# Token gathers of three graph layers in quarters of TensorE's array, two tiles at a time

## The reference, cut to what matters

```python
# layer 0: attention, 8 heads of 64
dots = where(m2, q @ k.T / 8, -big)
attn = 0.33 * softmax(dots) + 0.33 * adj + 0.33 * exp(-dist)     # masked; adj serves as dist too
x = LN(x + (attn @ v) @ W_out + b_out)
# layer 1: mean over neighbours
x = LN(x + relu(concat[x, (adj @ x) / deg] @ W.T))
# layer 2: two hypergraph convolutions, G = Dn * H @ (Be * H.T), H = (adj != 0)
h = LN(relu(G @ (x @ W1.T) + b1)) * gamma + beta
x = LN(x + (G @ (h @ W2.T) + b2 + x))
# layer 3: gated attention
xg = x * sigmoid(deg * Wd + bd)
s = (QK @ QK.T / 16) * adj,  QK = sigmoid(xg @ Wqk.T + bqk)
x = LN(x + relu((s / (sum(s) + 1e-6)) @ xg @ Wl.T + bl + xg @ Wr.T))
```

## Time and profile before

| | value |
|---|---|
| median of 3 runs | 1185.15 us |
| profiled execution, its own time | 1184.85 us |
| span of its instructions | 1182.8 us |
| TensorE (PE) busy | 1127.0 us, 95% |
| DVE busy | 919.8 us, 78% |
| ACT busy | 595.7 us, 50% |
| POOL busy | 572.5 us, 48% |

### The profile page before, as it was taken

The page is one execution under the profiler, slowest core; times in us unless marked ns, Lnnn a source line. Parts: engine busy times, 40 slices in busy tenths (PEclk is TensorE's granted clock), DMA queues, the critical chain, the costliest instruction groups (busy, mean ns, idle before and its releaser), DMA issues.

```text
span 1182.8 us, 29171 instructions
## 1 busy us (share of the span) xinstructions
PE 1127.0 (95%) x10416; PEld 951.4 (80%) x10416; DVE 919.8 (78%) x2223; ACT 595.7 (50%) x1266; POOL 572.5 (48%) x731
## 2 busy tenths in 40 slices
PE   5889999999999999999999999999999999999875
PEld 4768888888888888888888888888888888888763
DVE  6675887878788887878877788788778878777865
ACT  2536465454646445474544647454464645546331
POOL 2426356382644628264472735537273553826341
PEclk9899999999999999999999999999999999999897
DMA  7010102010010201001020100102001010100000
GB/s 233 24 28 1 46 3 67 1 48 21 22 44 0 67 0 44 22 22 44 0 67 0 43 24 22 44 0 67 0 23 44 18 49 0 42 8 28 2 23 18
DMA packets 52868, 37.22 MB, mean 31 GB/s; under 512 B 28182, under 2 KB 47707, under 8 KB 52827
## 3 DMA queue, kind: packets, MB, share of 16 engines
q1 hardware_dynamic: 51272, 35.09, 9.7%
q10 hardware_dynamic: 1554, 1.58, 0.5%
HBM read 28.27 MB, written 8.39 MB: 31 GB/s over the span
## 4 chain that ended last, share of the span: by engine, by line
PE 90%; DVE 5%; ACT 2%; POOL 1%; issue 1%; DMA 0%; SPq 0%; POOLq 0%; DVEq 0%; ACTq 0%
PE bank L1022 22%; PE bank L1024 21%; PE bank L1023 20%; PE bank L1093 3%; PE bank L1128 3%; PE bank L1163 2%; PE bank L1220 2%; PE bank L1201 2%; PE bank L1106 2%; PE bank L1294 2%; PE bank L1258 2%; DVE oT_lo L709 2%; PE bank L1083 1%; PE bank L1284 1%; PE bank L1248 1%; PE bank L1182 1%
## 5 line engine op out<-in xcount | busy, mean ns | idle before, releaser
L529 POOL TENSOR_TENSOR prob<-prob,srec 128x512 f32<-128x512 f32 x64 | 71.6, 1118 | 146.9 <-DVE srec L832 146.9
L467 POOL TENSOR_SCALAR var<-mv 128x2 f32<-128x2 f32 x128 | 29.0, 227 | 208.6 <-DVE mv L779 208.6
L786 DVE TENSOR_SCALAR x<-x,mv,rstd 128x256 f32<-128x256 f32 x256 | 119.0, 522 | 3.8 <-POOL rstd L470 3.3
L590 ACT ACTIVATE v<-bank 64x256 f32<-64x256 f32 x256 | 96.7, 378 | 17.7 <-PE bank L1024 15.4
L477 POOL TENSOR_TENSOR bhT<-hT,be 128x512 f32<-128x512 f32 x16 | 18.3, 1144 | 168.3 <-PE bank L1172 168.3
L775 DVE BATCH_NORM_STATS2 stats<-x 128x6 f32<-128x256 f32 x256 | 96.4, 418 | 4.4
L470 POOL TENSOR_TENSOR rstd<-var,negh 128x2 f32<-128x2 f32 x128 | 91.1, 712 | 10.7
L534 POOL TENSOR_TENSOR prob<-prob,mix 128x512 f32<-128x512 f32 x64 | 86.7, 1355 | 6.0 <-POOL prob L529 1.9
L918 DVE TENSOR_TENSOR hT_lo<-r,hT_hi 128x512 fp32r<-128x512 f32 x64 | 69.7, 1089 | 22.4 <-ACT hT_hi L633 22.2
L1022 PE MATMUL bank<-wo_hi,oT_hi 128*128 128x256 f32 x256 | 75.1, 293 | 8.9 <-DVE oT_lo L709 8.9
L1022 PE MATMUL bank<-w_hi,hT_hi 128*128 128x258 f32 x256 | 75.8, 296 | 2.7 <-DVE hT_lo L918 2.1
(11 more groups left out here) (202 smaller groups left out, 3697.9 us busy)
## 6 DMA issues: line engine op xcount, KB each, us to landing
xTin<-in_x_t SPq DMA_DIRECT2D x32, 256.0 KB, 2.8
xin<-in_x SPq DMA_DIRECT2D x16, 512.0 KB, 3.7
out_x<-x SPq DMA_DIRECT2D x32, 256.0 KB
adjA<-in_adj SPq DMA_DIRECT2D x16, 128.0 KB, 2.5
adjB<-in_adj_t SPq DMA_DIRECT2D x32, 64.0 KB, 3.1
adjC<-in_adj_t SPq DMA_DIRECT2D x32, 64.0 KB, 2.3
r<-in_wqkv ACTq DMA_DIRECT2D x2, 512.0 KB, 4.1
x<-in_wqkv SPq DMA_DIRECT2D x1, 512.0 KB, 8.2
```

What stands on the lines that cost most here:

```text
L529: pool.tensor_tensor(rows_of(u), rows_of(u), srec[:, k, :].rearrange("p (h a) -> p h a", a=1) .broadcast_to([P, 2 * HP, N]), ALU.mult).the ...
L590: ins = act.activation(v[e * N:(e + 1) * N, i, gr, :, :], src[gr * N:(gr + 1) * N, e], ACT.Copy)
L786: ins = dve.tensor_scalar(x[:, t, :], x[:, t, :], mv[layer][:, t, 0:1], rstd[layer][:, t:t + 1], ALU.subtract, ALU.mult)
```

## The change

1. `agg`, `agg3` and `hyper` take two tiles together and one matmul for each graph of each tile, with 64 rows and 64 columns of weights: the even tile's graphs go to their own partitions of one bank, the odd tile's graphs go crosswise into another bank, so four matmuls name four different quarters of the array. The readers on DVE follow: a pair of tiles is read by three instructions in place of one or two, one for the even tile and one for each half of the odd tile (`PARTS`).
2. `spread` uses one matmul for each graph (64 rows, 128 columns of weights, 64 columns moving), graph h into bank h, tile by tile; `up` then waits for both low parts.
3. `graph_c` multiplies the two diagonal blocks alone; DVE reads them by two instructions.
4. The mask rows stand twice, on partitions 0 to 3 and 64 to 67 (`MR` is 68), and `score` takes even and odd heads' masks from different rows, by turns.
5. The steps `agg` 1, `hyper` 1, `agg3` 1 and 3 and `spread` 1 of `PE_ORDER` do nothing now: their work is in the step before.
6. All four tables are new.

```diff
+PARTS = [(slice(0, P), slice(0, P), 0), (slice(0, N), slice(N, P), 1), (slice(N, P), slice(0, N), 1)]
 PE_ORDER = [
-    ("A", "k", 1), ("B", "turn1", 0), ("B", "turn1", 1), ("A", "k", 2), ("D", "turn3", 0), ("D", "turn3", 1),
+    ("A", "k", 1), ("B", "turn1", 0), ("B", "turn1", 1), ("D", "turn3", 0), ("D", "turn3", 1), ("B", "y1", 0),
...
+        def quarter(h, odd=0):
+            to = (h + odd) % 2
+            return slice(h * N, (h + 1) * N), slice(to * N, (to + 1) * N)
+        def graph_of(ap, h):
+            return ap[:, :, :].rearrange("p c (t a n) -> p c t a n", a=2, n=N)[:, :, :, h, :]
...
 # VectorE: agg (hyper and agg3 in the same way)
-                for k in range(2):
-                    ins = dve.scalar_tensor_tensor(out=xl[1][:, lo + k, :], in0=src[:, k * D:(k + 1) * D],
+                for rows, frm, odd in PARTS:
+                    ins = dve.scalar_tensor_tensor(out=xl[1][rows, lo + odd, :], in0=bank_of("agg", odd)[frm, i * D:(i + 1) * D],
...
 # TensorE: score
-                for e in range(2):
-                    for k in range(2):
-                        pe.matmul(dst[e][:, k * HP * N:(k + 1) * HP * N], mi[:, 2 * i + k, :],
+                for k in range(2):
+                    for e in range(2):
+                        rows = slice(e * N, e * N + 4)
+                        pe.matmul(dst[e][:, k * HP * N:(k + 1) * HP * N], mi[rows, 2 * i + k, :],
 # TensorE: graph_c
-                    ins = pe.matmul(dst[:, t * P:(t + 1) * P], hT0[:, t, :], bhT[:, t, :], start=True, stop=True)
+                    for h in range(2):
+                        at = slice(h * N, (h + 1) * N)
+                        ins = pe.matmul(dst[at, t * P + h * N:t * P + (h + 1) * N], hT0[at, t, at], bhT[at, t, at],
 # TensorE: agg
-                pe.wait_ge(*count("y1_ready", g, 2 * i + 2))
-                for k in range(2):
-                    ins = pe.matmul(dst[:, k * D:(k + 1) * D], adjB[:, 2 * i + k, :], yb[:, 2 * i + k, :], start=True, stop=True)
+                if i:
+                    return
...
+                for k in range(2):
+                    pe.wait_ge(*count("y1_ready", g, 2 * k + 2))
+                    for h in range(2):
+                        for odd in range(2):
+                            rows, to = quarter(h, odd)
+                            ins[odd] = pe.matmul(bank_of("agg", odd)[to, k * D:(k + 1) * D], adjB[rows, 2 * k + odd, rows],
+                                                 yb[rows, 2 * k + odd, :], start=True, stop=True, skip_group_check=True)
 # TensorE: spread
+                for t in range(T):
+                    for c in range(C):
+                        for h in range(2):
+                            rows = slice(h * N, (h + 1) * N)
+                            col = (c * T + t) * N
+                            ins[h] = pe.matmul(bank_of("spread", h)[:, col:col + N], xl[1][rows, t, c * P:(c + 1) * P],
+                                               gT[rows, t, rows], start=True, stop=True, skip_group_check=True)
 # TensorE: up
-                                 [count("spread_lo", g, c + 1) for c in range(C)]), "up", i)
+                                 [count("spread_lo", g, C) for c in range(C)]), "up", i)
```

More of the change, by code:

```diff
@@ L941, in hyper @@
                 lo, hi = 2 * i, 2 * i + 2
-                dve.wait_ge(*filled("hyper", i, g))
-                src = bank_of("hyper", i)
+                for odd in range(2):
+                    dve.wait_ge(*filled("hyper", odd, g))
+                    apart(dve, g)
                 dve.wait_ge(*count("x2_ready", g, 2))
                 dve.wait_ge(*count("out_done", g, 32, 1))
-                ins = dve.scalar_tensor_tensor(out=flat(xl[2][:, lo:hi, :]), in0=flat(xl[1][:, lo:hi, :]), scalar=2.0,
-                                               in1=src[:, :], op0=ALU.mult, op1=ALU.add)
+                for rows, frm, odd in PARTS:
+                    ins = dve.scalar_tensor_tensor(out=xl[2][rows, lo + odd, :], in0=xl[1][rows, lo + odd, :], scalar=2.0,
+                                                   in1=bank_of("hyper", odd)[frm, i * D:(i + 1) * D], op0=ALU.mult, op1=ALU.add)
                 ins.then_inc(SEM["sum2_ready"], 1)
@@ L1191, in graph_d @@
                 now_full(ins, "gT", 0)
-            def gathered(name, g, i, src, mat, halves=None):
-                pe.wait_ge(*emptied(name, i, g))
-                dst = bank_of(name, i)
-                for t in range(T):
-                    if halves and i == 0 and t % 2 == 0:
-                        pe.wait_ge(*count(halves, g, t // 2 + 1))
-                    ins = pe.matmul(dst[:, t * P:(t + 1) * P], src[:, t, i * P:(i + 1) * P], mat[:, t, :],
-                                    start=True, stop=True)
-                now_full(ins, name, i)
             def y1(g, i):
@@ L1252, in hyper @@
             def hyper(g, i):
-                pe.wait_ge(*count("down_ready", g, 2 * i + 2))
-                pe.wait_ge(*emptied("hyper", i, g))
-                dst = bank_of("hyper", i)
-                both(dst, 0)
-                for k in range(2):
-                    ins = pe.matmul(dst[:, k * D:(k + 1) * D], gT[:, 2 * i + k, :], yw[:, 2 * i + k, :], start=False,
-                                    stop=(k == 1), skip_group_check=True)
-                now_full(ins, "hyper", i)
+                if i:
+                    return
+                for odd in range(2):
+                    pe.wait_ge(*emptied("hyper", odd, g))
+                    both(bank_of("hyper", odd), 0)
+                ins = [None, None]
+                for k in range(2):
+                    pe.wait_ge(*count("down_ready", g, 2 * k + 2))
+                    apart(pe, g)
+                    for h in range(2):
+                        for odd in range(2):
+                            rows, to = quarter(h, odd)
+                            ins[odd] = pe.matmul(bank_of("hyper", odd)[to, k * D:(k + 1) * D], gT[rows, 2 * k + odd, rows],
+                                                 yw[rows, 2 * k + odd, :], start=False, stop=(k == 1), skip_group_check=True)
+                for odd in range(2):
+                    now_full(ins[odd], "hyper", odd)
             def qk(g, i):
@@ L1288, in agg3 @@
             def agg3(g, i):
+                if i % 2:
+                    return
                 pe.wait_ge(*count("sim_ready", g, 1))
-                pe.wait_ge(*count("y3_ready", g, i + 1))
+                pe.wait_ge(*count("y3_ready", g, i + 2))
                 apart(pe, g)
-                pe.wait_ge(*emptied("agg3", i, g))
-                now_full(pe.matmul(bank_of("agg3", i)[:, 0:D + 1], sT[:, i, :], yl[:, i, :], start=True, stop=True), "agg3", i)
+                for odd in range(2):
+                    pe.wait_ge(*emptied("agg3", i + odd, g))
+                    apart(pe, g)
+                ins = [None, None]
+                for h in range(2):
+                    for odd in range(2):
+                        rows, to = quarter(h, odd)
+                        ins[odd] = pe.matmul(bank_of("agg3", i + odd)[to, 0:D + 1], sT[rows, i + odd, rows], yl[rows, i + odd, :],
+                                             start=True, stop=True, skip_group_check=True)
+                for odd in range(2):
+                    now_full(ins[odd], "agg3", i + odd)
             steps = {
@@ L1323, with twice @@
     mrow[2:4, 1 + N:] = [[-BIG], [BIG]]
+    def twice(rows):
+        both = _np.zeros((MR,) + rows.shape[1:], rows.dtype)
+        both[0:4], both[N:N + 4] = rows, rows
+        return both
     m = a["nodemask"]
```

87 lines of the change are left out of this document (59 added, 28 removed), and 62 rows, old and new, of tables (ACT_ORDER, DVE_ORDER, PE_ORDER, POOL_ORDER).

## The result

| | before | after |
|---|---|---|
| median of 4 runs each, us | 1185.01 | 1231.12 |
| range of the runs | 1184.29 to 1186.23 | 1230.51 to 1234.55 |
| ratio, 95% interval | | 1.0394 (1.0373 to 1.0415) |
| span of the profiled execution | 1182.8 | 1228.7 |

The prediction was 1182, with a range of 1156 to 1198. It was wrong: the change costs 46 us. Executions come in a fast state and, rarely, a slow one at a lower granted clock; in what follows only one is slow, 1393.74 us for the kernel with the residual put back, and its figures are of its other three runs.

What follows compares the result with a forecast made beforehand. PE's streaming was taken as the bound: 67.6 us a round plus waits of 1.7, 0.15 and 0.3, less 0.2 for cheaper edges, gives 69.55, 0.25 under today; over 15 rounds 3 us less, so 1182 us, range 1156 to 1198.

Steps and rivals of the forecast that it cites:

- What PE is spared and pays: PE's round: 69.80 us, less 3.84 spared, plus 1.62 for changes of tiling, gives 67.6 without waits; no saving from `spread`.
- What DVE pays: Half-tile reads cost as much as full ones, 0.48 us; about 3.6 us more a round, 59.7 us of DVE work.
- The wait at `turnp` 0: PE, right behind `up` 3, waits for POOL's `soft` 1: 1.3 to 1.9 us a round, taken as 1.7.
- Smaller waits: PE waits 0.15 us at `agg` for ACT's copies of `y1` 3 and 0.3 more at `q` 0 for `split_low`.
- I keep to the rows: DVE's `hid_lo` slows POOL's `soft` 1 by 0.64 us in all, not the 1.3 of an exclusive port lock.
- The first 90 and last 116 us give nothing.: The run's start and end, outside the even rounds, are full of waits and bring no gain.
- slower by POOL: Rival, chance 0.18: POOL's `soft` 1 and `soft` 3 late, 0.6 us each; rounds of 70.8 us, 1200 us in all.
- 15 x 0.25: 15 rounds, each 0.25 us shorter than before (69.55 us), taken as 3 us saved in the run.

Runs made afterwards that it cites:

- the two kernels of the test: Changed kernel with residual and `graph_d` moved, with spread's matmuls, copies and `up`'s waits as in the kernel before, against the same with halves: 1218.66 us against 1218.8.
- the first experiment: Changed kernel with POOL's residual add put back behind `agg` 1 instead of first in POOL's table: 1224.04 us, ratio 1.0347 to the kernel before.

## Why the prediction was wrong

- **What PE is spared and pays.** Right. The prediction had 67.6 us for a round without waits, the trace has 67.3, by taking the waits off one round. Eight records of `agg3` take 592.16 - 591.57 = 0.59 us with an edge, and `agg` 1.28 for both pairs. Spread saved nothing. By the Trainium skill, "TensorEngine Tiling (Array Packing)", Theoretical Speedup, it could have run up to twice as fast; the trace shows nothing of that, 2.00 us for 32 records in the chain and no difference between the two kernels of the test.
- **What DVE pays.** The price of one operation was right: on 64 partitions it takes what it takes on 128.

```profile
L1017 DVE SCALAR_TENSOR_TENSOR yr<-bank,simrec,yr 64x256 f32<-64x256 f32 x64 | 30.9, 483 | 4.3 <-DVE simrec L1012 1.2
L1017 DVE SCALAR_TENSOR_TENSOR yr<-bank,simrec,yr 128x256 f32<-128x256 f32 x32 | 15.5, 484 | 3.8 <-DVE simrec L1012 1.1
```

  That the round's sum fits, 60.6 us for 59.7, is luck: 2.2 us of it are the long `yw`, which I hadn't seen. With the residual and `graph_d` moved it is 58.4, so the added work came to 2.3 us and not 3.6.
- **The wait at `turnp` 0.** Right in place and size: 1.62 us for 1.7, 15 times. The PE timeline of the changed kernel:

```profile
538.46 1.09 PE L1138 MATMUL bank<-ident,prob 128*128 128x128 f32 x8 [1.62 <-POOL prob L546]
```

- **"Smaller waits": this is the step that failed.** The mechanism at `turnp` was right; the sum of the other waits was not. I listed 0.45 us for `agg` and `q` 0. The trace has 3.3 us beside `turnp`: `turn3` 1.13, spread 0.58, `down` 0 about 0.5, `hyper`'s second pair about 0.6, and those two (0.15, an estimate, and 0.3). The missing 2.8 us a round are more than the 2.2 (69.80 - 67.6) that I had the code spare. I had followed only one chain, to `turnp`, and had taken all other steps of the new tables as free of waits because the old ones were. The runs show three of the missing ones: POOL's residual against DVE's `yw`, `gT`'s copy without `v` 1 behind it, and `hid_lo` without `score` 1 in front of `down`.
- **"I keep to the rows" on the port pair.** Right for `soft` 1, too narrow as a rule. The Trainium skill, "SBUF — State Buffer", Who interferes with whom, has the lock exclusive for the whole instruction; the trace agrees, with a `yw` of 2.90 us beside a POOL instruction of 2.39. I weighed it in one place and didn't look for others: the table moved POOL's longest instruction to the front of its order, and the tables of the change showed that. The rounds of the first experiment tell it from both sides: whichever started first took its usual time, and the other took longer.
- **"The first 90 and last 116 us give nothing."** They gave a loss: 5.6 and 12.2 us. Between the 15th and the 16th spread, where stream N is gone and PE has less to put into gaps, PE waits 11.4 us where it waited 5.1, by the lists of waits of both. The granted clock is a little lower there too, 0.93 and then 0.82 to the end, where it was 0.94 and 0.85. I measured no edit for these parts alone.
- **The rival "slower by POOL"** had the right sign and was given 0.18, with another mechanism and at most 1200.
- **A slip in the sum.** 15 x 0.25 is 3.75 us and not 3; the forecast would have been 1181. It changes nothing.

What the experiments settle of the 46 us: residual and `graph_d` give back 12. Taking `score` 1 out of the gap ahead of `down` costs the old kernel 26. Giving it back to the changed kernel, with its shifts, gains nothing: `up` 0 and `turnp` 2 wait instead. So the rest isn't one wait. That it is a shortage of PE work for two gaps is my reading; the test for it, `score` 1 back together with whole-array `spread`, of which `up` 0 could take one half after the other, was not made. How the remaining 34 us divide between DVE's longer steps and the order was not separated; no table tried here got the new code below 1217.

## What to carry to other kernels

- When a hand-written order is new, follow every chain through it and ask of each step what used to stand between producer and consumer. A chain that showed no wait before may have had cover; price the step by the cover's length and the producer's lateness, not by its old wait.
- Work that is spared just ahead of a step that is only just ready is handed back there. This kernel, at 95% PE, gains only where the follower has slack.
- Of a change with code and tables together, try the parts that need no new order first. Here they gave 0.5% and the whole cost 4%.
